# Two-layer LoRA kernel: product 5 of the first span taken by output tile

## The chip, the cores and the metric

The kernel runs on one core of a Trainium2 chip. The metric is the device time of one execution in microseconds (us), as the median over timed runs. Before the change it is 404.14 us (three runs, 402.94 to 404.2 us).

## The reference, cut to what matters

Two layers with a residual each, in float32, on x of 8 batches x 256 tokens x 1024 features:

```
# layer 0
base   = x @ W.T                                   # 1024 x 1024
logits = x @ Wr.T;  logits[.., language] += 5      # 8 experts
gates  = softmax over the top 2 logits, scattered to 8 experts
h      = x @ A.T                                   # 8 experts x rank 16 = 128
x      = x + base + 2 * (h * gates) @ B            # B: 128 x 1024
# layer 1
x      = x + x @ weight[adapter of the batch].T    # 1024 x 1024, chosen per batch
```

## The kernel before, in words

**Precision.** Every large product is made from parts: ScalarE copies an operand to float32r ("high", line 965), VectorE subtracts the copy from the operand ("low", line 583), and TensorE adds high x high, high x low and low x high (the function `step`, lines 1227 to 1229, three matmuls of 128x128 by 512 columns). The identity is added to the weights, so the residual needs no operation of its own.

**Layer 0.** The 2048 tokens go in two spans of 1024 (s = 0, 1). In a span the 1024 x 1024 by 1024 product is done in Strassen's way (Winograd's form) with seven products of 512 x 512 by 512, in the order 1, 2, 6, 7, 5, 4, 3. Each product has four slices k of the contraction and four output tiles r, one PSUM bank per tile: 16 steps, 48 matmuls. "By tile" means that r is the outer loop and k the inner one, so that tile r ends after 4(r+1) steps; otherwise k is outer and all four tiles end in the last four steps. `by_tile` says which: before, products 1, 2 and 6 of span 0. `product_end` and `k_end` turn that into counts of the semaphore `steps`. Products 1, 6, 7 and 4 accumulate in the four "main" banks, products 2, 5 and 3 in the four "side" banks. Sums between products are taken out of PSUM: `copy_u3` (ScalarE, L1007) copies a main bank after product 7, `add_up` (VectorE, L715) adds a side bank to a kept sum and gives one output tile of a quarter of the result (C11, C22, C12), and `keep` (issued from ScalarE's queue, L1017) stores that tile in DRAM. `copy_u2` (L1002) copies main banks after product 6.

**The operands of product 5** are sums as well: S1 (L628, VectorE, one per tile r, in place in the weights) gives the weight side, pieces ("u", 5, r); the token side is pieces ("x", 0, 5, k). The other made operands around are T4 (L620) and D of B (L623, `sum_bd`, with the piece ("bd",), used by the LoRA term of C12 at the end of the span).

**The LoRA term.** VectorE makes the gates (`make_gates`, L650 to L687), TensorE turns h x gates (L1259), ScalarE and VectorE split it (`gT_high` L987, `gT_low` L692), and TensorE adds three matmuls per tile into the bank (`lora`, L1238 to L1241). For C11 that comes between products 7 and 5: the four side banks get the LoRA term, `add_up` reads them, and only then may product 5 begin in the same banks.

**The order around the change** is written by hand, one in-order program per engine. Semaphores `hi_done` and `lo_done` count the pieces, and the list PIECES gives each piece its number, so ScalarE and VectorE must make them in that order. Before, VectorE ended its work ahead of product 5 in this order: gates, low of B, S1(0), gT_low, S1(1), S1(2), low u5(0), S1(3), low u5(1 to 3), low x5(0), the four sums of C11, low x5(1 to 3), D of B, T4 x4, low of D of B, low u4, low x4, the sums of C22. TensorE waited ahead of product 5 for all four u5 pieces and x5(0) (`whole_piece`), and ahead of each tile's first step for its sum of C11.

**Layer 1** then takes the eight batches one after another, each with a 1024 x 1024 weight loaded by DMA, turned and split in the same way (L730, L736, L1066), with its matmuls on lines 1349 to 1351.

Of the kernel before, what the change touches and what calls it, by code (L numbers as in the profile page):

```python
# [5 lines left out]
def cond_resid_kernel(nc, x, lang_ids, adapter_ids, w0, wr, a, b, w1, out):  # L6
# [15 lines left out]
    HM = M // 2  # L22
# [23 lines left out]


    def by_tile(s, i):
        return s == 0 and i in (1, 2, 6)

    def product_end(s, i, r=HM - 1):
        first = 16 * (7 * s + AT[i])
# [44 lines left out]
    PIECES += [("xr", t) for t in range(XT)] + [("wr", 0)]  # L97
    PIECES += [("x", 0, 6, t) for t in range(XT)] + [("u", 6, r) for r in range(HM)]
    PIECES += [("u", 7, r) for r in range(HM)] + [("x", 0, 7, k) for k in range(HM)] + [("b",)]
    for i in (5, 4, 3):  # L100
        PIECES += [("bd",)] if i == 4 else []
        PIECES += [("u", i, r) for r in range(HM)] + [("x", 0, i, k) for k in range(HM)]
    for i in ORDER:
        PIECES += [("x", 1, i, k) for k in range(HM)]
    PIECE_AT = {p: k for k, p in enumerate(PIECES)}
# [21 lines left out]
    with ctx:  # L127
# [407 lines left out]
        def _(dve):  # L535
# [38 lines left out]
            def low(p):  # L574
                dve.wait_ge(hi_done, PIECE_AT[p] + 1)
                if p[0] == "u" and p[1] == 4:
                    dve.wait_ge(s1_done, p[2] + 1)
                if p[0] == "u" and p[1] == 7:
                    dve.wait_ge(s2_done, p[2] + 1)
                if p[0] == "x" and p[2] == 3:  # L580
                    dve.wait_ge(t3_done, (p[1] + 1) * XT)
                _, high_part, low_part = sides(p)
                nc.vector.tensor_tensor(low_part, sides(p)[0], high_part.bitcast(F32), ALU.subtract).then_inc(lo_done, 1)  # L583
# [38 lines left out]
            def sum_bd():  # L622
                nc.vector.tensor_tensor(bd_sum, b_whole[:, 0:HALF], b_whole[:, HALF:D], ALU.subtract)\  # L623
                    .then_inc(bd_summed, 1)

            def make_s1(r):
                a21, a22 = quarter_w(5, r), quarter_w(4, r)
                nc.vector.tensor_tensor(a21, a21, a22, ALU.add).then_inc(s1_done, 1)  # L628
# [61 lines left out]
            def gT_low(s):  # L690
                dve.wait_ge(gT_hi_done, s + 1)
                nc.vector.tensor_tensor(gT_lo, gT_ps(s), gT_hi.bitcast(F32), ALU.subtract).then_inc(gT_done, 1)  # L692
# [6 lines left out]
            def add_up(s, quarter, r):  # L699

                dve.wait_ge(lora_done, quarter_at(s, quarter, r) + 1)
                if quarter == "11":
                    if r < DRAINED:
                        dve.wait_ge(p1_added, DRAINED * s + r + 1)
                    else:
                        dve.wait_ge(p1_copied, HM * s + r + 1)
                elif quarter == "22":
                    dve.wait_ge(u3_copied, HM * s + r + 1)
                else:
                    dve.wait_ge(u2_copied, HM * s + r + 1)  # L710
                e = quarter_at(s, quarter, r)
                if KEPT <= e < quarter_at(1, "12", 0):
                    dve.wait_ge(kept[e % KEPT], e // KEPT * 16)
                part = (sums2 if quarter == "12" else sums13)[:, r]
                nc.vector.tensor_tensor(kept_slot(e), side_bank(s, r), part, ALU.add).then_inc(summed_up, 1)  # L715
# [99 lines left out]
            make_gates(0)  # L815
            low(("b",))
            make_s1(0)
            gT_low(0)
            make_s1(1)
            make_s1(2)  # L820
            low(("u", 5, 0))
            make_s1(3)
            for r in range(1, HM):
                low(("u", 5, r))

            def span(s):
                low(("x", s, 5, 0))
                for r in range(HM):
                    add_up(s, "11", r)
                low(("x", s, 5, 1))  # L830
                low(("x", s, 5, 2))
                low(("x", s, 5, 3))
                if s:
                    turn_w1(0)
                    turn_w1(1)
                    low_w1(0)
                    turn_w1(2)
                    low_w1(1)
                    turn_w1(3)
                else:  # L840
                    sum_bd()
                    for t in range(XT):
                        make_t4(0, t)
                    low(("bd",))
                    lows("u", 4)
                lows("x", s, 4)
                if s:
                    low_w1(2)
                    turn_w1(4)
                    low_w1(3)  # L850
                    turn_w1(5)
                for r in range(HM):
                    add_up(s, "22", r)
                if s == 0:
                    lows("u", 3)
                lows("x", s, 3)
                if s == 0:
                    for t in range(XT):
                        turn(x_item(1, 0, t))
                else:  # L860
                    low_w1(4)
                    turn_w1(6)
                    low_w1(5)
                    turn_w1(7)
                    low_w1(6)
                    low_w1(7)
# [43 lines left out]
        def _(act):  # L910
# [56 lines left out]
            def highs(kind, *which):  # L967
                for r in range(HM):
                    high((kind, *which, r))
# [9 lines left out]
            def exponentials(s):  # L979
                act.wait_ge(drop_ready, s + 1)  # L980
                nc.scalar.activation(second[:], drop[:], ACT.Exp).then_inc(second_ready, 1)
# [137 lines left out]
            for q in range(Q):  # L1119
# [1 line left out]
                                     b_ps().rearrange("p a f -> p (a f)")  # L1121
                                     .rearrange("p (j q m h) -> p q m h j", j=M, q=Q, m=M)[:, q],
                                     ACT.Copy).then_inc(b_copied, 1)
            copy_u2(0, 0)
            copy_u2(0, 1)
            high(("x", 0, 7, 0))
            high(("x", 0, 7, 1))
            copy_u2(0, 2)
            copy_u2(0, 3)
            high(("x", 0, 7, 2))  # L1130
            high(("x", 0, 7, 3))
            high(("b",))
            exponentials(0)
            gT_high(0)

            def span(s):
                if s == 0:
                    highs("u", 5)
                highs("x", s, 5)
                for r in range(HM):  # L1140
                    copy_u3(s, r)
                keep_all(s, "11")
                if s:
                    for n in range(4):
                        high_w1(n)
                else:
                    high(("bd",))
                    highs("u", 4)
                highs("x", s, 4)
                keep_all(s, "22")  # L1150
                if s == 0:
                    highs("u", 3)
                highs("x", s, 3)
                if s:
                    load_x1(0)
                    load_x1(1)
                    high_w1(4)
                    high_w1(5)
                for r in range(HM):
                    copy_c21(s, r)  # L1160
                if s == 0:
                    keep_all(s, "21")
                else:
                    high_w1(6)
                    high_w1(7)
                    x1_high(0)
# [36 lines left out]
        def _(pe):  # L1203
# [64 lines left out]
            def first_products():  # L1268
# [12 lines left out]
                for r in range(HM):  # L1281
# [4 lines left out]
                    if r == 1:  # L1286
                        turn_b()

            def product(s, i, wait_bank, first, bank, ks=range(HM)):
                for k in ks:  # L1290
                    whole_piece(s, i, k)
                    for r in range(HM):
                        if k == 0:
                            wait_bank(r)
                        step(s, i, k, r, bank(s, r), first)

            def span(s):
                if s:
                    product(s, 6, lambda r: pe.wait_ge(p1_copied, HM * s + r + 1), False, main_bank)
                gated = 2 if s else 3  # L1300
                product(s, 7, lambda r: pe.wait_ge(u2_copied, HM * s + r + 1), False, main_bank, range(gated))
                turn_gated(s)
                product(s, 7, None, False, main_bank, range(gated, HM))
                pe.wait_ge(gT_done, s + 1)
                pe.wait_ge(lo_done, PIECE_AT["b",] + 1)
                for r in range(HM):
                    lora(s, "11", r)
                product(s, 5, lambda r: pe.wait_ge(summed_up, added_at(s, "11", r) + 1), True, side_bank)
                for r in range(HM):
                    lora(s, "22", r)  # L1310
                product(s, 4, lambda r: pe.wait_ge(u3_copied, HM * s + r + 1), False, main_bank)
                for r in range(HM):
                    lora(s, "21", r)
                product(s, 3, lambda r: pe.wait_ge(summed_up, added_at(s, "22", r) + 1), False, side_bank)
                pe.wait_ge(lo_done, PIECE_AT["bd",] + 1)
                for r in range(HM):
                    lora(s, "12", r)
# [61 lines left out]
```

## Time and profile before

| what | us |
|---|---|
| median of the timed runs | 404.14 |
| the profiled execution's own time | 401.46 |
| its span | 399.7 |
| PE busy (98% of the span) | 391.1 |
| DVE busy (78%) | 310.2 |
| ACT busy (43%) | 173.8 |

The profile is of one execution. PE is TensorE's matmuls, PEld its weight loads, DVE is VectorE, ACT is ScalarE, POOL is GpSimd, SP is the queue of most loads. ACTq is ScalarE's instruction queue, where it issues DMAs. A matmul's record is 0.39 us long, while the next one may start sooner. Starts are counted from the start of the span, and a later wait is named with the instruction that ended it.

### The profile page before, as it was taken

What the parts mean: (1) busy time and instruction counts of PE and PEld (TensorE: products, weight loads), DVE (VectorE), ACT (ScalarE), POOL (GpSimd) and SP (SyncE); (2) the same over time, 40 slices, a digit from 0 to 9 for tenths busy, and PEclk for the clock granted to TensorE, in tenths of its full rate; (3) what the DMA queues carried; (4) which work ended last, traced back from release to release, by engine and by line L of the source; (5) the groups of instructions that cost most, each with busy time, mean ns of one, the idle gap of its engine ahead of it and who ended that gap; (6) DMA issues with size and microseconds to landing.
All of it is one profiled execution on the core that took longest, in us unless ns stands there. A gap on an engine that the chain in (4) does not pass through costs nothing.

```text
span 399.7 us, 5958 instructions
## 1 busy us (share of the span) xinstructions
PE 391.1 (98%) x1900; PEld 330.0 (83%) x1900; DVE 310.2 (78%) x419; ACT 173.8 (43%) x245; POOL 52.9 (13%) x81
## 2 busy tenths in 40 slices
PE   8899999799999999999999999999999999999996
PEld 8698988588889888888888888878888888888886
DVE  5899998997457568229877956999999999999900
ACT  3352263754220143335355333655555555656511
POOL 1005300000000100000110211442232120323000
PEclk9999999999999999999999999999999999999999
DMA  9998750033476400006492999999999999999232
GB/s 208 227 200 209 106 161 2 0 107 106 137 202 204 91 1 0 2 0 197 136 289 117 229 261 247 281 250 267 271 274 282 266 277 282 272 260 235 66 93 52
DMA packets 87553, 68.60 MB, mean 172 GB/s; under 512 B 16322, under 2 KB 86498, under 8 KB 87010
## 3 DMA queue, kind: packets, MB, share of 16 engines
q1 hardware_dynamic: 60832, 46.55, 49.8%
q10 hardware_dynamic: 26690, 21.67, 18.3%
q8 instruction: 15, 0.25, 0.3%
q14 instruction: 16, 0.13, 0.1%
HBM read 53.51 MB, written 14.68 MB: 171 GB/s over the span
## 4 chain that ended last, share of the span: by engine, by line
PE 94%; DVE 2%; ACT 1%; DMA 1%; issue 0%; ACTq 0%; DVEq 0%
PE banks L1349 15%; PE banks L1350 15%; PE banks L1351 15%; PE banks L1227 13%; PE banks L1228 12%; PE banks L1229 12%; PE banks L1220 7%; PE banks L1238 2%; PE banks L1240 2%; PE banks L1241 2%; DMA turned_w_f<-in_x_dram 1%; DVE weights L583 1%; ACT weights L965 0%; DVE turned_w_f L628 0%; PE banks L1259 0%; DVE tokens_f L545 0%
## 5 line engine op out<-in xcount | busy, mean ns | idle before, releaser
L1227 PE MATMUL banks<-ring,weights 128*128 128x512 f32 x192 | 75.2, 392 | 2.4 <-DVE stage L715 2.4
L1349 PE MATMUL banks<-weights,tokens 128*128 128x512 f32 (+1 forms) x184 | 70.0, 380 | 0.0
L1351 PE MATMUL banks<-weights,tokens 128*128 128x512 f32 (+1 forms) x184 | 69.9, 380 | 0.0
L1350 PE MATMUL banks<-weights,tokens 128*128 128x512 f32 (+1 forms) x184 | 69.9, 380 | 0.0
L1066 ACT ACTIVATE weights<-weights_f 128x1024 fp32r<-128x1024 f32 x44 | 46.5, 1060 | 52.7 <-DVE weights_f L730 49.8
L730 DVE STREAM_TRANSPOSE weights_f<-raw 128x1024 f32<-128x1024 f32 x42 | 51.8, 1235 | 6.1 <-POOL raw L501 5.6
L501 POOL TENSOR_TENSOR raw<-raw,ident 128x128 f32<-128x128 f32 x42 | 26.0, 619 | 216.0 <-DMA raw<-in_L_cond_weight_dram 216.0
L736 DVE TENSOR_TENSOR weights<-weights_f,weights 128x1024 fp32r<-128x1024 f32 x44 | 52.3, 1190 | 0.9 <-ACT weights L1066 0.9
L1229 PE MATMUL banks<-ring,turned_w 128*128 128x512 f32 x128 | 49.8, 389 | 0.0
L1228 PE MATMUL banks<-tokens,weights 128*128 128x512 f32 x128 | 49.8, 389 | 0.0
L1227 PEld LDWEIGHTS banks<-ring,weights 128*128 128x128 f32 x192 | 36.0, 188 | 10.1 <-DVE tokens L583 2.8
L1349 PEld LDWEIGHTS banks<-weights,tokens 128*128 128x128 f32 x184 | 34.6, 188 | 7.0 <-issue 0.4
L1351 PEld LDWEIGHTS banks<-weights,tokens 128*128 128x128 f32 x184 | 34.6, 188 | 6.6
L1350 PEld LDWEIGHTS banks<-weights,tokens 128*128 128x128 f32 x184 | 34.6, 188 | 6.5
L965 ACT ACTIVATE ring<-tokens_f 128x512 fp32r<-128x512 f32 x40 | 22.5, 621 | 29.2 <-PE banks L1229 25.1
L1066 ACT ACTIVATE turned_w<-weights_f 128x1024 fp32r<-128x1024 f32 x20 | 21.2, 1060 | 23.6 <-DVE weights_f L730 23.5
L1349 PE MATMUL banks<-turned_w,tokens 128*128 128x512 f32 x80 | 31.1, 389 | 0.0
L1350 PE MATMUL banks<-turned_w,tokens 128*128 128x512 f32 x80 | 31.1, 389 | 0.0
L1351 PE MATMUL banks<-turned_w,tokens 128*128 128x512 f32 x80 | 31.1, 389 | 0.0
L730 DVE STREAM_TRANSPOSE weights_f<-ring_f 128x1024 f32<-128x1024 f32 x22 | 27.1, 1233 | 5.1 <-POOL ring_f L501 5.1
L1220 PEld LDWEIGHTS banks<-fac,tokens_f 128*128 128x128 f32 x256 | 30.0, 190 | 0.3
L1220 PE MATMUL banks<-fac,tokens_f 128*128 128x136 f32 x256 | 30.1, 279 | 0.0
(127 smaller groups left out, 613.8 us busy)
## 6 DMA issues: line engine op xcount, KB each, us to landing
raw<-in_L_cond_weight_dram SPq DMA_DIRECT2D x168, 128.0 KB, 5.2
ring_f<-in_L_cond_weight_dram SPq DMA_DIRECT2D x88, 128.0 KB, 5.8
out_dram<-sums ACTq DMA_DIRECT2D x31, 256.0 KB, 7.0
raw<-in_x_dram SPq DMA_DIRECT2D x48, 128.0 KB, 3.7
x_kept<-stage ACTq DMA_DIRECT2D x24, 256.0 KB, 3.2
raw<-in_L_cond_W_dram SPq DMA_DIRECT2D x16, 128.0 KB, 3.2
turned_w_f<-in_x_dram SPq DMA_DIRECT2D x12, 128.0 KB, 6.6
ring_f<-in_L_cond_W_dram SPq DMA_DIRECT2D x12, 128.0 KB, 5.4
```

The source lines that it names most:

```text
L501: nc.gpsimd.tensor_tensor(spot, spot, ident[:].rearrange("p (q j) -> p q j", q=Q), ALU.add)\
L730: nc.vector.transpose(w1_turn(n).rearrange("p (m q s) -> p q m s", m=M, q=Q), raw_tile(SLOT[item]).rearrange("p (q m j) -> p q m j", q=Q, ...
L736: nc.vector.tensor_tensor(w1_dest(n, 1), w1_turn(n).rearrange("p (m f) -> p m f", m=M), w1_dest(n, 0).bitcast(F32), ALU.subtract).then_inc ...
L965: nc.scalar.activation(sides(p)[1], sides(p)[0], ACT.Copy).then_inc(hi_done, 1)
L1066: nc.scalar.activation(w1_dest(n, 0), w1_turn(n).rearrange("p (m f) -> p m f", m=M), ACT.Copy)\
L1220: mm = nc.tensor.matmul(ps, xT[:, m, :], fac[:, m, 0:FC], start=m == 0, stop=m == M - 1)
L1227: nc.tensor.matmul(ps, u_hi, x_hi, start=first and k == 0, stop=False, skip_group_check=True)
L1228: nc.tensor.matmul(ps, u_hi, x_lo, start=False, stop=False, skip_group_check=True)
L1229: nc.tensor.matmul(ps, u_lo, x_hi, start=False, stop=k == HM - 1, skip_group_check=True)\
L1349: nc.tensor.matmul(ps, x_hi, w_hi, start=m == 0, stop=False)
L1350: nc.tensor.matmul(ps, x_hi, w_lo, start=False, stop=False)
L1351: mm = nc.tensor.matmul(ps, x_lo, w_hi, start=False, stop=m == M - 1)
```

## The change

Product 5 of span 0 goes by output tile (`product_5`), and tile r waits for ("u", 5, r) and its own sum of C11 alone. VectorE makes x5(0) right after S1(0), and then one set per tile: the sum of C11, S1 and the piece u5. ScalarE makes the x parts of product 7 before its last `copy_u2`, x5(0) before `gT_high`, and `copy_u3` and `keep` of C11 tile by tile. D of B and its parts come after the x parts of product 4 rather than before product 4's parts. Span 1 keeps its order.

```diff
     def by_tile(s, i):
-        return s == 0 and i in (1, 2, 6)
+        return s == 0 and i in (1, 2, 6, 5)
@@ PIECES
-    for i in (5, 4, 3):
+    PIECES += [("x", 0, 5, 0), ("u", 5, 0)] + [("x", 0, 5, k) for k in range(1, HM)] + [("u", 5, r) for r in range(1, HM)]
+    for i in (4, 3):
+        PIECES += [("u", i, r) for r in range(HM)] + [("x", 0, i, k) for k in range(HM)]
         PIECES += [("bd",)] if i == 4 else []
-        PIECES += [("u", i, r) for r in range(HM)] + [("x", 0, i, k) for k in range(HM)]
@@ VectorE
             make_gates(0)
             low(("b",))
             make_s1(0)
+            low(("x", 0, 5, 0))
             gT_low(0)
+            low(("u", 5, 0))
+            low(("x", 0, 5, 1))
+            add_up(0, "11", 0)
+            low(("x", 0, 5, 2))
+            low(("x", 0, 5, 3))
             make_s1(1)
             make_s1(2)
-            low(("u", 5, 0))
+            low(("u", 5, 1))
+            add_up(0, "11", 1)
             make_s1(3)
-            for r in range(1, HM):
-                low(("u", 5, r))
+            low(("u", 5, 2))
+            add_up(0, "11", 2)
+            low(("u", 5, 3))
+            add_up(0, "11", 3)
 
             def span(s):
-                low(("x", s, 5, 0))
-                for r in range(HM):
-                    add_up(s, "11", r)
-                low(("x", s, 5, 1))
-                low(("x", s, 5, 2))
-                low(("x", s, 5, 3))
                 if s:
+                    low(("x", s, 5, 0))
+                    for r in range(HM):
+                        add_up(s, "11", r)
+                    low(("x", s, 5, 1))
+                    low(("x", s, 5, 2))
+                    low(("x", s, 5, 3))
...
                 else:
-                    sum_bd()
                     for t in range(XT):
                         make_t4(0, t)
-                    low(("bd",))
                     lows("u", 4)
                 lows("x", s, 4)
...
+                else:
+                    sum_bd()
+                    low(("bd",))
                 for r in range(HM):
                     add_up(s, "22", r)
@@ ScalarE
-            copy_u2(0, 0)
-            copy_u2(0, 1)
-            high(("x", 0, 7, 0))
-            high(("x", 0, 7, 1))
-            copy_u2(0, 2)
+            for r in range(HM - 1):
+                copy_u2(0, r)
+            highs("x", 0, 7)
             copy_u2(0, 3)
-            high(("x", 0, 7, 2))
-            high(("x", 0, 7, 3))
             high(("b",))
             exponentials(0)
+            high(("x", 0, 5, 0))
             gT_high(0)
+            high(("u", 5, 0))
+            for k in range(1, HM):
+                high(("x", 0, 5, k))
+            for r in range(1, HM):
+                high(("u", 5, r))
+                copy_u3(0, r - 1)
+                keep(0, "11", r - 1)
+            copy_u3(0, HM - 1)
+            keep(0, "11", HM - 1)
 
             def span(s):
-                if s == 0:
-                    highs("u", 5)
-                highs("x", s, 5)
-                for r in range(HM):
-                    copy_u3(s, r)
-                keep_all(s, "11")
                 if s:
+                    highs("x", s, 5)
+                    for r in range(HM):
+                        copy_u3(s, r)
+                    keep_all(s, "11")
                     for n in range(4):
                         high_w1(n)
                 else:
-                    high(("bd",))
                     highs("u", 4)
                 highs("x", s, 4)
+                if s == 0:
+                    high(("bd",))
                 keep_all(s, "22")
@@ TensorE
+            def product_5():
+                for r in range(HM):
+                    pe.wait_ge(lo_done, PIECE_AT["u", 5, r] + 1)
+                    pe.wait_ge(summed_up, added_at(0, "11", r) + 1)
+                    for k in range(HM):
+                        if r == 0 and k:
+                            pe.wait_ge(lo_done, PIECE_AT["x", 0, 5, k] + 1)
+                        step(0, 5, k, r, side_bank(0, r), True)
...
-                product(s, 5, lambda r: pe.wait_ge(summed_up, added_at(s, "11", r) + 1), True, side_bank)
+                if s:
+                    product(s, 5, lambda r: pe.wait_ge(summed_up, added_at(s, "11", r) + 1), True, side_bank)
+                else:
+                    product_5()
```

## Rows read from the trace of the kernel before

**Rows 1.** The page's parts 1 and 4: busy time, and the chain by engine.
```profile
PE 391.1 (98%) x1900; PEld 330.0 (83%) x1900; DVE 310.2 (78%) x419; ACT 173.8 (43%) x245; POOL 52.9 (13%) x81
PE 94%; DVE 2%; ACT 1%; DMA 1%; issue 0%; ACTq 0%; DVEq 0%
```
**Rows 2.** TensorE's waits: who waited for whom, total us, times, longest.
```profile
PE banks L1227 <- DVE stage L715: 2.4, 1, 2.4
PE banks L1206 <- POOL ident L490: 1.7, 1, 1.7
PE banks L1227 <- DVE weights L583: 1.3, 1, 1.3
```
**Rows 3.** Timeline of TensorE, matmuls: start, us, engine, line.
```profile
58.65 0.39 PE L1229 MATMUL banks<-ring,weights 128*128 128x512 f32 x1
60.92 0.39 PE L1227 MATMUL banks<-ring,weights 128*128 128x512 f32 x1
...
73.18 0.39 PE L1241 MATMUL banks<-lora_g,lora_b 128*128 128x512 f32 x1
...
75.22 0.39 PE L1241 MATMUL banks<-lora_g,lora_b 128*128 128x512 f32 x1
78.00 0.47 PE L1227 MATMUL banks<-ring,weights 128*128 128x512 f32 x1 [2.40 <-DVE stage L715]
78.31 0.40 PE L1228 MATMUL banks<-tokens,weights 128*128 128x512 f32 x1
...
88.99 0.39 PE L1238 MATMUL banks<-lora_g,lora_b 128*128 128x512 f32 x1
91.71 0.39 PE L1227 MATMUL banks<-ring,weights 128*128 128x512 f32 x1
```
**Rows 4.** Timeline of VectorE, neighbours of one form merged (xcount).
```profile
59.80 1.29 DVE L583 TENSOR_TENSOR tokens<-tokens_f,ring 128x512 fp32r<-128x512 f32 x2 [0.25 <-ACT ring L965]
62.27 1.29 DVE L583 TENSOR_TENSOR tokens<-tokens_f,ring 128x512 fp32r<-128x512 f32 x2 [1.17 <-ACT ring L965]
...
67.56 1.22 DVE L687 TENSOR_TENSOR stage<-stage 128x1024 f32<-128x1024 f32 x1
...
71.22 1.22 DVE L692 TENSOR_TENSOR lora_g<-banks,lora_g 128x1024 fp32r<-128x1024 f32 x1 [0.70 <-ACT lora_g L987]
72.36 1.28 DVE L628 TENSOR_TENSOR turned_w_f<-turned_w_f 128x512 f32<-128x512 f32 x2
...
76.57 0.69 DVE L583 TENSOR_TENSOR tokens<-tokens_f,ring 128x512 fp32r<-128x512 f32 x1
77.17 2.48 DVE L715 TENSOR_TENSOR stage<-banks,sums 128x512 f32<-128x512 f32 x4
...
87.64 2.49 DVE L583 TENSOR_TENSOR tokens<-tokens_f,ring 128x512 fp32r<-128x512 f32 x4
```
**Rows 5.** Timeline of ScalarE, the same columns.
```profile
59.14 1.16 ACT L965 ACTIVATE ring<-tokens_f 128x512 fp32r<-128x512 f32 x2 [1.28 <-PE banks L1229]
60.20 0.58 ACT L1002 ACTIVATE sums<-banks 128x512 f32<-128x512 f32 x1
...
70.16 1.03 ACT L987 ACTIVATE lora_g<-banks 128x1024 fp32r<-128x1024 f32 x1 [5.22 <-PE banks L1259]
...
73.08 1.23 ACT L965 ACTIVATE weights<-turned_w_f 128x512 fp32r<-128x512 f32 x2 [1.37 <-DVE turned_w_f L628]
```
**Rows 6.** ScalarE's DMA issues of `keep`: duration ns min/median/max.
```profile
L1017 ACTq DMA_DIRECT2D x_kept<-stage x24: 366/424/1112, 79.8 to 202.9; - x24
```
**Rows 7.** Busy time by stretch: PE, PEld, DVE, ACT, POOL, granted clock, DMA share, GB/s.
```profile
75.50:78.00 2.50, 0.11 (x1) 0.03 (x1) 2.50 (x5) 2.14 (x6) 0.00 (x0) 1.00 0.00 0
78.00:400.00 322.00, 318.48 (x1492) 266.86 (x1492) 241.54 (x285) 140.27 (x186) 42.45 (x64) 1.00 0.69 178
```

## The prediction

> **What bounds the kernel now.** I read the page first, then TensorE's waits, then the timelines of the three engines around the longest of them. The page gives PE 391.1 us of a span of 399.7, and the chain of waits runs 94% over PE [rows 1]. So TensorE sets the time, and only what takes idle time out of it, or puts some in, counts. Its waits are three [rows 2]: two at the start of the span, which the change does not touch, and one of 2.4 us for an `add_up` (L715). The timeline places that one between the LoRA term of C11 and product 5: a matmul starts at 75.22, the next only at 78.00 [rows 3]. VectorE is busy in every part of 75.50 to 78.00, ScalarE in 2.14 us of 2.50 [rows 7]: it is not data that is late but VectorE's order, which makes four u5 pieces and x5(0) before the first sum. That sum is the instruction at 77.17, and it releases TensorE [rows 4].
>
> **What the gap costs.** Product 5 has 48 matmuls and is followed by the 12 of the LoRA term of C22, from 88.99 to 91.71 [rows 3]: 2.72/12 = 0.2267 us each when nothing waits. Without the gap product 5 would begin at 75.22 + 0.227 = 75.45 and end 48 x 0.2267 = 10.88 later, at 86.33. It ends at 88.99. The gap is worth 2.66 us, a little more than the 2.4 of the waits, since matmuls restart slowly (78.00 to 78.31 is 0.31, not 0.23). This is the most that the change can give; by tile or by slice the matmuls are as many and of the same shape. By-tile order brings no cost of its own: product 6 is by tile and its last ten steps run from 58.65 to 60.92 at 2.27/10 = 0.227 [rows 3].
>
> **Before product 5.** ScalarE now does copy_u2(2) before x7(0). It stood idle 1.28 us before x7(0) at 59.14 [rows 5], and that x part waits for product 6's step at 58.65 + 0.39 = 59.04. Tile 2 of product 6 ends three matmuls sooner, about 58.36, so the copy (0.58) runs about 58.40 to 58.98, in that idle time, and x7(0) stays near 59.14. This matters, since TensorE starts product 7 at 60.92 and the low part starts at 59.80 [rows 3, 4] and ends 0.69 later, at 60.49: some 0.1 us to spare before the weight load that goes ahead of the matmul. I cost it at nothing; if ScalarE were late by d, it costs d less 0.1. x7(2) and x7(3) move from behind two copies to before the last. Then x7's lows end about 1.4 us sooner (start 62.27 before, about 60.9 after), and the gates with them: 67.56 + 1.22 = 68.78 becomes about 67.4. TensorE turns the gated h only after three slices of product 7, at 69.09 in any case, so this gives no time, and gT_high stays at 70.16 [rows 5] and gT_low at 71.22. What it gives is room: VectorE has x5(0)'s low and S1(0) done by 69.8 and waits for gT_low at 71.22 [rows 4]. copy_u2(3) moves by about 0.2 us to 61.3 and is needed at 62.6 (product 7's tenth matmul): covered.
>
> **Product 5, step by step.** VectorE starts successive instructions of 128x512 0.60 us apart although each lasts 0.69 (four in 2.48, so 2.48 - 0.69 over 3) [rows 4]. ScalarE's high follows the S1 it needs by 0.03 (72.36 + 0.69 = 73.05, start 73.08 [rows 4, 5]), lasts 0.63, and the low follows by 0.03. From the end of a sum to the second matmul of the tile it releases takes 78.31 - (77.17 + 0.69) = 0.45.
> From 72.36: low u5(0) 72.36, low x5(1) 72.96, sum 0 at 73.61 (its LoRA matmul starts at 73.18 and ends 0.39 later [rows 3]), low x5(2) 74.21, low x5(3) 74.81, S1(1) 75.41, S1(2) 76.01. High u5(1) runs 76.13 to 76.76, so low u5(1) starts 76.79 and sum 1 at 77.39, ending 78.07. S1(3) 77.99, low u5(2) 78.59, sum 2 at 79.19 ends 79.87; low u5(3) 80.15, sum 3 at 80.75 ends 81.43. ScalarE has between these a copy_u3 (0.6) and a keep, whose issue takes 0.42 at the median [rows 6], per tile; with both, high u5(2) is ready at 78.4 and high u5(3) at 80.1, as used.
> TensorE: tile 0 needs sum 0 by 75.2 and has it at 74.3. Tile 1's second matmul is due at 75.45 + 13 x 0.2267 = 78.40; the sum allows 78.07 + 0.45 = 78.52. So 0.12 is lost, with 0.02 of restart: 0.15. Tile 2 needs its sum by 80.8 (79.87) and tile 3 by 83.5 (81.43). Gain 2.66 - 0.15 = 2.5.
> The one added wait that can bind is thus tile 1's. Behind it on TensorE is everything. Its cost lies between 0 (VectorE 0.15 quicker) and the 0.7 of the first rival.
>
> **Behind product 5.** It now ends at 86.5, and product 4 begins after 12 LoRA matmuls at 89.2 (91.71 before [rows 3]). T4 x4 starts at 81.35; ScalarE's u4 highs wait for all T4 and start at 83.9, VectorE's u4 lows at 84.5 and x4(0)'s at 86.9, ending 87.6 (before 87.64 + 0.69 = 88.3 [rows 4]). Needed at about 88.9: 1.3 us of room, where there were 3.2. D of B, its high and its low (0.69, 0.63, 0.69) then stand between x4 and the sums of C22, which end at 93.8; the keeps and u3's parts queue behind them and are complete at 97.5, x3(0) at 98.1, against product 3's start near 102.7. Product 5 by tile frees its banks no later, and D of B itself is first used at the end of product 3. Nothing later has a date that does not follow TensorE: the loads of span 1 and the weights of layer 1 wait for slots that are freed behind TensorE's steps, and from 78 to 400 PE has no wait in the list [rows 2, 7]. The gain should stay whole.
>
> **Rule weighed.** The four sums of C11 take 2.48 us with 0.69 for one, so the next starts before the last has ended [rows 4].
> The Trainium skill ("VectorE: DVE Perf Modes", section "The DRAIN you can't avoid") says that the next operation starts only when the pipe has emptied, and lets instructions that are not held start sooner. This trace agrees with the second half; by the first alone the chain would be that of the first rival.
>
> **Rivals.**
> 1. *The tile 1 chain is slower than its neighbours suggest*: with no overlap each VectorE instruction takes 0.69 from start to start, counted from gT_low's end at 72.44. Six of them to the end of S1(1) give 76.58, high u5(1) ends 77.24, S1(2) 77.27, low u5(1) and sum 1 end at 78.65, second matmul 79.10 instead of 78.40: 0.7 lost, gain 1.9, time 402.2. For it: many semaphore handoffs in a new order; against it: the pitch of every merged row. 0.13.
> 2. *No change*: the time is given back later (product 4's 1.3 us of room used up by a late T4 or u4, or the start of product 7 late by d), leaving under 1.2. It needs two of these covers to fail together by over 1.5 us; time 403.6. Speaking for it only that DVE is full from 71 to 90. 0.12.
> 3. *Slower*: the chain per tile paces product 5. Place: tiles 1 to 3. If nothing overlaps and each keep takes the longest issue seen, a tile costs S1 0.69, high 0.63, copy 0.60, issue 1.11 [rows 6], low 0.69, sum 0.69 and 0.1 of handoffs = 4.5 against 2.72 of matmuls; three tiles lose 5.4, less the head start of 0.9 that tile 0's sum has: 4.5, so 1.8 more than the gain, time 406. It decides from 2.72 + 0.9 = 3.6 us per tile on. Against it: the S1s of tiles 2 and 3 are made ahead, and the engines overlap. 0.05.
> That the change does not do what it says I see no way to: the new waits are per tile.
> My forecast has 0.70.
>
> **The numbers.** The profiled execution took 401.46 us, 1.76 above its span; it would take 401.46 - 2.5 = 398.96. The median of the runs shown is 2.68 above the profiled one. Applied to the median, 404.14 - 2.5 = 401.6. The runs spread by 1.3 us, and the lowest less the whole gap is 402.94 - 2.66 = 400.3, the lower end. The upper end takes in rival 1 and part of rival 2: 403.5. About 0.3% (1.2 us) is what a measurement of this kernel tells from no change. Faster: forecast and rival 1, less a little for the spread of the runs, 0.80; same 0.14; slower 0.06.
>
> **What would show it.** Right: in the changed profile TensorE's wait for L715 near 75 is gone or below 0.3 us; product 5's first matmul starts near 75.45, the LoRA term of C22 near 86.5 and product 4 near 89.2; gates' last instruction ends near 67.4; VectorE's first sum of C11 starts near 73.6 and the second near 77.4. Wrong: a new wait on an L583 piece or on L715 at tiles 1 to 3, a gap at 60.9 (product 7) or at 89 (product 4), or a span that is not 2.5 us shorter though the gap is gone.

## The result, and the profile after

| | before | after |
|---|---|---|
| median of the timed runs, us | 403.6 (6 runs, 401.41 to 404.6) | 399.35 (6 runs, 398.84 to 399.8) |
| profiled execution, us | 401.46 | 398.99 |
| its span, us | 399.7 | 397.2 |

The ratio is 0.9899 (95% interval 0.9872 to 0.9926), so the change is faster by 4 us. The forecast was 401.6 with a range of 400.3 to 403.5: the time lies below it. Yet between the two profiled executions the difference is 2.5 us, which is the gain of the forecast. Both facts hold, and the question of the experiments is where the other 1.7 us are.

TensorE's waits in the changed kernel (who waited for whom, us in total, times, longest; L1243, L584 and L716 are L1227, L583 and L715 of before). The wait of 2.4 us [rows 2] is gone:

```profile
PE banks L1222 <- POOL ident L491: 1.7, 1, 1.7
PE banks L1243 <- DVE weights L584: 1.7, 1, 1.7
```

The timeline of its matmuls where [rows 3] had the standstill, and at the ends of products 5 and of the LoRA term:

```profile
75.29 0.39 PE L1257 MATMUL banks<-lora_g,lora_b 128*128 128x512 f32 x1
75.52 0.39 PE L1243 MATMUL banks<-ring,weights 128*128 128x512 f32 x1
...
78.01 0.39 PE L1245 MATMUL banks<-ring,turned_w 128*128 128x512 f32 x1
78.32 0.47 PE L1243 MATMUL banks<-ring,weights 128*128 128x512 f32 x1
78.62 0.40 PE L1244 MATMUL banks<-tokens,weights 128*128 128x512 f32 x1
...
86.57 0.39 PE L1254 MATMUL banks<-lora_g,lora_b 128*128 128x512 f32 x1
...
89.29 0.39 PE L1243 MATMUL banks<-ring,weights 128*128 128x512 f32 x1
```

Product 5 follows the LoRA term at once (75.52, forecast 75.45). Tile 1 starts at 78.32, 0.31 behind its predecessor instead of 0.23, and its second matmul follows after 0.30: 0.15 lost, as worked out. Product 4 starts at 89.29 against 91.71, 2.42 sooner.

VectorE's chain for the same stretch, against [rows 4]:

```profile
66.38 1.23 DVE L688 TENSOR_TENSOR stage<-stage 128x1024 f32<-128x1024 f32 x1
...
71.29 1.22 DVE L693 TENSOR_TENSOR lora_g<-banks,lora_g 128x1024 fp32r<-128x1024 f32 x1 [1.35 <-ACT lora_g L998]
...
73.68 0.69 DVE L716 TENSOR_TENSOR stage<-banks,sums 128x512 f32<-128x512 f32 x1
...
77.49 0.68 DVE L716 TENSOR_TENSOR stage<-banks,sums 128x512 f32<-128x512 f32 x1
...
80.49 0.69 DVE L716 TENSOR_TENSOR stage<-banks,sums 128x512 f32<-128x512 f32 x1
...
86.75 2.49 DVE L584 TENSOR_TENSOR tokens<-tokens_f,ring 128x512 fp32r<-128x512 f32 x4
```

The gates end at 67.6 (forecast 67.4), the first, second and fourth sum of C11 start at 73.68, 77.49 and 80.49 (73.6, 77.4, 80.75), the low part of x4(0) at 86.75 (86.9). ScalarE, against [rows 5], has its copy of tile 2 in what was idle time, and x7(0) stays where it was next to its step:

```profile
58.47 0.60 ACT L1013 ACTIVATE sums<-banks 128x512 f32<-128x512 f32 x1 [0.54 <-PE banks L1245]
59.21 2.20 ACT L976 ACTIVATE ring<-tokens_f 128x512 fp32r<-128x512 f32 x4
```

So nothing in the schedule differs from the forecast by more than 0.3 us. What differs is the kernel before: its profiled execution was not a typical one.

### The profile page after: what moved, and what is told of

Same layout as the page of the kernel before. It is cut to its first block, busy times and chain, and to the rows that moved or that the text cites. A ratio compares the mean times of both kernels' runs of the same rounds, so it can differ in the third digit from the quotient of the medians.

```text
span 397.2 us, 5961 instructions
## 1 busy us (share of the span) xinstructions
PE 390.6 (98%) x1900; PEld 330.0 (83%) x1900; DVE 311.2 (78%) x419; ACT 173.6 (44%) x245; POOL 55.2 (14%) x81
## 4 chain that ended last, share of the span: by engine, by line
PE 96%; DVE 1%; DMA 1%; ACT 1%; ACTq 0%; issue 0%; DVEq 0%
PE banks L1377 15%; PE banks L1378 15%; PE banks L1379 15%; PE banks L1243 13%; PE banks L1244 13%; PE banks L1245 13%; PE banks L1236 7%; PE banks L1256 2%; PE banks L1254 2%; PE banks L1257 2%; DMA turned_w_f<-in_x_dram 1%; DVE weights L584 1%; ACT weights L976 0%; PE banks L1275 0%; DVE tokens_f L546 0%; PE banks L1265 0%
## 5 line engine op out<-in xcount | busy, mean ns | idle before, releaser
L1243 PE MATMUL banks<-ring,weights 128*128 128x512 f32 x192 | 75.5, 393 | 0.0
L502 POOL TENSOR_TENSOR raw<-raw,ident 128x128 f32<-128x128 f32 x42 | 30.3, 722 | 218.3 <-DMA raw<-in_L_cond_weight_dram 218.3
L1243 PEld LDWEIGHTS banks<-ring,weights 128*128 128x128 f32 x192 | 36.1, 188 | 7.9 <-issue 0.3
L1245 PEld LDWEIGHTS banks<-ring,turned_w 128*128 128x128 f32 x128 | 24.0, 188 | 5.0
```

The costliest lines, as they stand in the source:

```text
L502: nc.gpsimd.tensor_tensor(spot, spot, ident[:].rearrange("p (q j) -> p q j", q=Q), ALU.add)\
L1243: nc.tensor.matmul(ps, u_hi, x_hi, start=first and k == 0, stop=False, skip_group_check=True)
L1245: nc.tensor.matmul(ps, u_lo, x_hi, start=False, stop=k == HM - 1, skip_group_check=True)\
```

## The experiments

In each experiment the kernel before was timed on the same chip, and every timed run lists its mean granted clock of TensorE. Counts of runs below are counts of these lists.

**1. The kernel before again.** No edit.

> The kernel before, unchanged, profiled and timed once more. What is asked: the changed kernel's profile shows just the 2.5 us of the forecast (span 397.2 against 399.7), yet the timed runs moved by 4.1 us (ratio 0.990), because most runs of the kernel before took 403 to 404.6 us while the profiled one took 401.46. Theory T1 (a thin cover in the kernel before gives way in most runs: TensorE's turn of h x gates has 0.1 us of room there and 1.3 us after the change): a slower execution shows TensorE waiting at L1259, for 1 to 3 us. Rival T2 (the scatter lies elsewhere, in the loads of the start or of layer 1, and has nothing to do with the change): a slower execution shows its extra time at the start or behind 222 us, with the stretch from 55 to 105 us as in the first profile.

Measured: 403.04 us, ratio 0.9994 (0.9975 to 1.0012). Its profiled execution is a slower one, 403.03 us with a span of 401.2, and shows no wait at L1259 (T1) and nothing new at either end of the span (T2). TensorE's waits are those of [rows 2], the standstill is as long as before, and what follows it is not. Busy time by stretch; the column behind POOL is the granted clock, in this second profile of the kernel before:

```profile
76.00:78.00 2.00, 0.00 (x0) 0.00 (x0) 2.00 (x5) 1.81 (x4) 0.00 (x0) 1.00 0.00 0
78.00:80.00 2.00, 1.78 (x5) 1.42 (x6) 2.00 (x5) 1.83 (x4) 0.00 (x0) 0.59 0.00 0
80.00:82.00 2.00, 2.00 (x7) 1.57 (x6) 2.00 (x4) 0.56 (x1) 0.00 (x0) 0.55 0.54 176
82.00:84.00 2.00, 2.00 (x10) 1.64 (x9) 2.00 (x5) 0.64 (x1) 0.00 (x0) 1.00 1.00 343
```

And its matmuls:

```profile
75.43 0.39 PE L1241 MATMUL banks<-lora_g,lora_b 128*128 128x512 f32 x1
78.22 0.64 PE L1227 MATMUL banks<-ring,weights 128*128 128x512 f32 x1 [2.40 <-DVE stage L715]
78.66 0.63 PE L1228 MATMUL banks<-tokens,weights 128*128 128x512 f32 x1
79.08 0.63 PE L1229 MATMUL banks<-ring,turned_w 128*128 128x512 f32 x1
...
81.22 0.63 PE L1228 MATMUL banks<-tokens,weights 128*128 128x512 f32 x1
81.64 0.46 PE L1229 MATMUL banks<-ring,turned_w 128*128 128x512 f32 x1
81.94 0.40 PE L1227 MATMUL banks<-ring,weights 128*128 128x512 f32 x1
...
90.80 0.39 PE L1238 MATMUL banks<-lora_g,lora_b 128*128 128x512 f32 x1
```

After standing still from 75.66 to 78.22, TensorE works at its lower clock, 1.2 GHz: the first eight matmuls of product 5 take 3.42 us (78.22 to 81.64), 0.427 each instead of 0.227. Then the clock is back at 2.4 GHz. Product 5 takes 90.80 - 78.22 = 12.58 us against 88.99 - 78.00 = 10.99 in [rows 3]: 1.6 us more. Half a clock missing for 3.42 us of 401.2 makes a mean clock of 0.996 over the whole execution, which is what this run lists. In all experiments together 78 runs of the kernel before were listed: 56 have a clock of 0.996 or less, with a median of 403.2 us, and 22 have 0.998 to 1.0, with a median of 401.6. The first profile, with 401.46 us and a clock of 1.00, is like the 22. T1 and T2 both fall, and a third theory, T3, takes their place: the standstill brings the clock down in about 7 executions of 10. So far this is an inference from one profile; experiments 5 to 8 test it.
The Trainium skill ("TensorE: Matmul & The Clock Gate", section "Part 1: The HAM clock gate (the "warmup" mystery)") says that TensorE's clock gate passes only half of the pulses after it has been idle. The trace agrees: the granted clock is 0.59 and 0.55 in the two stretches behind the standstill.

**2. ScalarE's order around product 7 alone**, in the kernel before:

```diff
-            copy_u2(0, 0)
-            copy_u2(0, 1)
-            high(("x", 0, 7, 0))
-            high(("x", 0, 7, 1))
-            copy_u2(0, 2)
+            for r in range(HM - 1):
+                copy_u2(0, r)
+            highs("x", 0, 7)
             copy_u2(0, 3)
-            high(("x", 0, 7, 2))
-            high(("x", 0, 7, 3))
```

> The kernel before with only ScalarE's new order around product 7 (copy_u2(0 to 2), the four x7 parts, copy_u2(3)). In the profile the gap ahead of product 5 stays 2.66 us and the gates end at 67.4 instead of 68.8. T1: the median falls by 1 to 1.6 us (ratio about 0.997), with runs that scatter less. T2: ratio 1.000.

Measured: 403.03 us (401.27 to 405.0), ratio 0.9994 (0.9976 to 1.0012), 9 of 12 runs at 0.996 or less. No gain and no smaller scatter: room for the gates is worth nothing by itself. T1 is rejected.

Its profile (403.04 us) has the same standstill of 2.55 us, from 75.34 to 77.89, and the clock falls behind it too, but later:

```profile
77.89 0.47 PE L1223 MATMUL banks<-ring,weights 128*128 128x512 f32 x1 [2.40 <-DVE stage L715]
...
79.13 0.45 PE L1225 MATMUL banks<-ring,turned_w 128*128 128x512 f32 x1
79.38 0.63 PE L1223 MATMUL banks<-ring,weights 128*128 128x512 f32 x1
...
82.77 0.40 PE L1225 MATMUL banks<-ring,turned_w 128*128 128x512 f32 x1
```

Here the first six matmuls of product 5 are 0.25 apart, and only the next eight (79.38 to 82.77, 0.424 each) run at the lower clock. The granted clock falls to 0.50 at 79.3, 1.4 us after TensorE has begun to work again; in the profile of experiment 1 it is 1.00 through the whole standstill as well and falls at 78.4, 0.2 us after the first matmul.

**3. The changed kernel with ScalarE's old order there** (the same edit the other way round).

> The changed kernel with ScalarE's old order around product 7. The gates end at 68.8, and S1(0) and x5(0) just fit before gT_low at 71.3, so the span stays near 397.2. T1: the median is 1 to 1.6 us above the changed kernel's (ratio to before about 0.993, the forecast's 2.5 us), and runs scatter as before. T2: ratio as the changed kernel's, 0.990.

Measured: 399.31 us, ratio 0.9906 (0.989 to 0.9923), span 397.4, no run below 0.999. That is the changed kernel's time (399.35), so nothing else in the change needs this part.

**4. D of B back where it was**, in the changed kernel:

```diff
                 else:
+                    sum_bd()
                     for t in range(XT):
                         make_t4(0, t)
+                    low(("bd",))
                     lows("u", 4)
...
-                else:
-                    sum_bd()
-                    low(("bd",))
```

> The changed kernel with D of B made where it was (sum before T4, its low before u4). VectorE is then 1.2 us later at u4 and x4(0), about 88.8, and product 4 wants x4(0) at about 88.9 (it starts at 89.3 in the changed kernel): a wait of 0 to 0.5 us, ratio to before 0.990 to 0.991. Both theories alike; it prices the part 'D of B later'.

Measured: 399.49 us, ratio 0.9917 (0.9895 to 0.9939), span 397.4. x4(0)'s low starts at 87.71 instead of 86.75 and ends at 88.40, and TensorE has no wait at product 4, so the 1.3 us of room were enough for it. One of its six runs is at 401.04 us with a clock of 0.995, though this kernel has no standstill ahead of product 5; its profile is of another run (clock 1.0) and does not explain it. What the part gives is below what can be told here.

**5. The standstill filled**, in the kernel before; product 5 starts as late as it did, but TensorE is at work until then.

```diff
                 for r in range(HM):
                     lora(s, "11", r)
+                if s == 0:
+                    for _ in range(10):
+                        extra = nc.tensor.matmul(main_bank(0, HM - 1), bT_hi[:, 0:P], gT_hi[:, 0, :], start=False,
+                                                 stop=True, skip_group_check=True)
+                    extra.then_inc(filled, 1)
```

(ScalarE's copy of that bank waits for `filled`. The ten matmuls add to the bank what does not belong there, so the kernel serves for timing only.)

> The kernel before with ten more matmuls of 128x128 by 512 after the LoRA term of C11, in the bank of tile 3 of product 7 (they add to C11, C12 and C21 of that tile what does not belong there), so that TensorE works for 2.27 us of the 2.55 it stood still. VectorE's chain and the start of product 5 at 78.0 us stay. What is asked: in most runs of the kernel before the granted clock is 0.996 instead of 1.0, and its second profile shows product 5's first eight matmuls 0.427 us apart instead of 0.227 (1.2 GHz), right behind the standstill. Theory T3 (the standstill brings the clock down): no run falls to 0.996, all are near 401.3 us, ratio 0.995. Rival T4 (the clock falls at this point for another reason, and the changed kernel only happens to be spared): the share of runs at 0.996 stays as before (about 7 in 10), ratio 1.000.

Measured: 401.47 us (12 runs, 401.31 to 401.8), ratio 0.9969 (0.9954 to 0.9984); all 12 runs at 0.999 or 1.0, beside 21 of 32 runs of the kernel before at 0.996 or less. The profile of this kernel: ten matmuls that serve nothing, and product 5 behind them, 0.31 and then 0.23 apart, at a granted clock of 1.00.

```profile
75.89 2.43 PE L1313 MATMUL banks<-lora_g,lora_b 128*128 128x512 f32 x10
78.44 0.47 PE L1230 MATMUL banks<-ring,weights 128*128 128x512 f32 x1
78.75 0.39 PE L1231 MATMUL banks<-tokens,weights 128*128 128x512 f32 x1
```

Ten useless matmuls make the kernel before faster by 1.2 us (the ratio) to 1.5 us (the medians). The rival T4 falls: only TensorE's standstill was taken away.

**6 and 7. A standstill put into the changed kernel**, by one wait ahead of product 5:

```diff
             def product_5():
+                pe.wait_ge(s1_done, 3)                                 # only in 6
+                pe.wait_ge(summed_up, added_at(0, "11", 1) + 1)        # only in 7
```

> The changed kernel, where product 5 waits also for S1 of tile 2 (made at 76.8 us): TensorE stands still from 75.5 to 76.9, 1.3 us. T3: the clock falls in fewer runs than with 2.6 us of standstill, perhaps none; span +1.3 to 1.4, median 400.7, ratio 0.993 to 0.994. T4: no fall.

> The changed kernel, where product 5 waits also for the sum of C11 of tile 1 (77.49 + 0.69 = 78.2 us): TensorE stands still for 2.75 us, as long as in the kernel before, while all else is the changed kernel. Only 2.6 us of standstill come back (the 0.2 us wait ahead of tile 1 goes). T3: 7 in 10 runs at clock 0.996 with 1.7 us more, median at that of the kernel before, 403.3, ratio 1.000. T4: no fall, median 401.9, ratio 0.9965.

Measured for 6: 400.67 us, ratio 0.9948 (0.9929 to 0.9967), nine runs, none below 0.998: 1.3 us above the changed kernel's 399.4 in the other comparisons, and 1.3 us is the length of its standstill (75.64 to 76.94), so nothing more is lost. Measured for 7: 403.34 us, ratio 1.0004 (0.9985 to 1.0022), 8 of 12 runs at 0.996 or less. A standstill of 2.70 us (75.50 to 78.20) brings back the time of the kernel before, with everything else as changed. The eight runs with the lower clock have a median of 403.5 us, the four others 401.9. In its profile the stretches around the standstill:

```profile
76.00:78.00 2.00, 0.00 (x0) 0.00 (x0) 1.90 (x4) 1.63 (x3) 0.00 (x0) 1.00 0.38 129
78.00:80.00 2.00, 1.80 (x4) 1.46 (x5) 2.00 (x5) 1.17 (x2) 0.00 (x0) 0.57 0.40 133
80.00:82.00 2.00, 2.00 (x7) 1.55 (x6) 2.00 (x4) 1.20 (x2) 0.00 (x0) 0.58 0.39 132
```

**8. x5(0) early, product 5 by slice.** The kernel before with the edit of experiment 2 and x5(0) made ahead of gT_low (with its high ahead of gT_high, and its number in PIECES):

```diff
             make_s1(0)
+            low(("x", 0, 5, 0))
             gT_low(0)
```

> The kernel before with ScalarE's new order around product 7 and x5(0) made before gT_high and gT_low, as in the changed kernel; product 5 goes by slice and S1, u5 and the sums keep their order. One VectorE instruction of 0.60 us leaves the chain ahead of the first sum: standstill 1.95 us instead of 2.55, span -0.6. T3: the clock falls in fewer runs, so the median falls by more than 0.6: 400.8 to 402.7, ratio 0.994 to 0.9985. T4: -0.6 alone, ratio 0.9985.

Measured: 400.96 us (12 runs, 400.71 to 401.95), ratio 0.9955 (0.9941 to 0.9968), no run below 0.999. Its matmuls at the standstill:

```profile
75.14 0.39 PE L1244 MATMUL banks<-lora_g,lora_b 128*128 128x512 f32 x1
77.32 0.47 PE L1230 MATMUL banks<-ring,weights 128*128 128x512 f32 x1 [1.79 <-DVE stage L716]
```

From 75.37 to 77.32 is 1.95 us. With ScalarE's order of experiment 2, which alone gave nothing, moving one instruction of 0.60 us away from the sums gives 1.8 us (0.45%), somewhat under half of what the whole change gives: 0.6 from the shorter standstill (the runs of before that kept their clock have a median of 401.6, which is 0.65 above 400.96), the rest because the clock no longer falls. The profiled run is one of the slower ones, 401.58; it has a wait of 0.74 us for a token part at 194.72 that the profile before doesn't have.

**9. The changed kernel again.**

> The changed kernel once more, for more executions. T3 (the standstill of 2.6 us ahead of product 5 brings the clock down, and the change gains the standstill and the slow matmuls behind it): no run at a granted clock of 0.996 or less, median 399.3, ratio to before 0.990 to 0.992 as before runs at 0.996 are two thirds or more; against the runs of before that stayed at 1.0 (401.2 to 401.9) the gain is the 2.5 us of the forecast. T4 (chance): some runs at 0.996.

Measured: 399.45 us, ratio 0.9914 (0.9889 to 0.9939), all six runs at 0.999 or 1.0, beside 8 of 11 of the kernel before at 0.996 or less. Those three of before that stayed up took 401.25 to 401.92 us: 1.8 to 2.5 us more.

**10. S1 of tile 1 sooner**, in the changed kernel:

```diff
             add_up(0, "11", 0)
+            make_s1(1)
             low(("x", 0, 5, 2))
             low(("x", 0, 5, 3))
-            make_s1(1)
-            make_s1(2)
             low(("u", 5, 1))
             add_up(0, "11", 1)
+            make_s1(2)
```

> The changed kernel with S1 of tile 1 made right after the first sum, ahead of x5(2) and x5(3), and S1 of tile 2 after the second sum. High u5(1) is then ready at 75.6, the sum of tile 1 starts at 76.7 instead of 77.5, and the 0.07 us wait with its restart (0.15 in all) ahead of tile 1 goes; x5(2) starts at 74.9, wanted at 76.9. Span 397.0, median 0.1 to 0.2 below the changed kernel's, less than the measurement can tell.

Measured: 399.08 us against 399.45 for the changed kernel in the same comparison; ratios to before 0.9909 (0.9883 to 0.9934) and 0.9914, so the two can't be told apart by time. In the profile (span 396.8) tile 1's sum starts early enough that its matmul at 78.18 follows at 0.23, and product 5 takes 86.34 - 75.46 = 10.88 us, the 48 x 0.2267 of the forecast without any loss:

```profile
75.46 0.39 PE L1243 MATMUL banks<-ring,weights 128*128 128x512 f32 x1
...
78.18 0.39 PE L1243 MATMUL banks<-ring,weights 128*128 128x512 f32 x1
...
86.34 0.39 PE L1254 MATMUL banks<-lora_g,lora_b 128*128 128x512 f32 x1
```

## Why the prediction was right or wrong

**Right: the schedule.** The standstill's 2.66 us, the 0.15 us left at tile 1, the 1.3 us of room at product 4 (D of B later), the cover of copy_u2(2), and that nothing behind gives the gain back: the profiled spans differ by 2.5 us as worked out. Rival 1 (no overlap on VectorE) is excluded by the second sum at 77.49, rival 3 by the fourth at 80.49, rival 2 by product 4 at 89.29 and by the span, which keeps the gain to the end. That the early x7 parts give room but no time was right too (experiments 2 and 3). One word is wrong and changes nothing: what runs from 58.65 to 60.92 are the last ten matmuls of product 6, not ten steps.

**Wrong: a term that was left out.** The step that failed is the sentence in "What the gap costs": "The gap is worth 2.66 us ... This is the most that the change can give". In about 7 executions of 10 the same standstill also halves TensorE's clock for some 3.4 us behind it, and that costs 1.6 us more (12.58 against 10.99 us for product 5). So the gain on a typical execution is 2.5 + 1.6 = 4.1 us. The measured difference of the medians is 403.6 - 399.35 = 4.25. From the longer lists it is 403.2 (the 56 runs of before at the lower clock) - 399.4 (the 12 of the changed kernel) = 3.8, and without the clock's part, 401.6 (the 22 that stayed up) - 399.4 = 2.2. Where in an execution the clock falls is seen in three profiles (experiments 1, 2 and 7), each time behind the standstill; of the other runs only the mean clock and the time are known, and both fit. Experiment 5 takes the clock's part alone away (ratio 0.9969), experiment 7 puts both back (ratio 1.0004), experiment 6 shows a shorter standstill that costs its own length only.

Of the 2.25 us between the forecast of 401.6 and the 399.35 measured, this term is 1.6. Another 0.5 was in the starting point: the median of three runs was 404.14, that of six is 403.6 (and that of the 56 is 403.2). The lower end of the range, 402.94 - 2.66 = 400.3, lacks the same term.

**Why it was missed.** The trace of before showed the clock at 1.00 on both sides of the gap [rows 7], and I took that execution for the kernel. (Behind the gap that row is a mean over 322 us, in which 3.4 us at half clock would be 0.5%; it is the 10.99 us of product 5 that show that this execution had no fall.) But the forecast itself notes that the median of the runs shown is 2.68 us above the profiled execution, and passes over it as spread, by moving the result up with it: 404.14 - 2.5. The runs were 402.94, 404.2 and 404.14 and the profiled one 401.46. A profile faster than every run beside it may be from the faster of two groups, and the standstill of [rows 2, 3] was its one long one behind the start. Both together suggest a rival that the prediction should have had: what makes the typical run longer than the profiled one hangs on the gap and goes with it. Its time needs no further price: it is the profiled execution less the gain, 401.46 - 2.5 = 398.96, which stands in the prediction and was put aside for 401.6. Measured: 399.35.

**What stays open.** Why the clock stays up in 3 of 10 runs with the same standstill was not tried, nor why the fall came at once in two profiles and later in that of experiment 2, nor where one run of experiment 4 lost its clock. Within one group the runs of before still spread by about 1 us. TensorE's waits for VectorE's first weights (L583, 1.1 and 1.3 us in two profiles of before, 1.7 after) vary by part of that; I did not follow it further.

## What to carry to other kernels

A wait of TensorE costs its length and, from some length on, what the next matmuls lose at the lower clock; here 2.6 us of standstill cost about 4 in most executions, 1.95 us cost nothing beyond itself. So shortening a wait can pay more than it removes, and filling it with work that serves nothing can pay as well. Before a gain is worked out from one profile, compare that execution's time and clock with the timed runs: where they form two groups, ask which group the profile shows and what the change does to the other.

## What the hardware showed unexpectedly

How often the clock falls changed within a narrow range of the standstill's length, with matmuls of the same shape on both sides. Runs at a mean clock of 0.996 or less: none of 12 in the changed kernel (no standstill there) and one of 18 in its variants without a standstill (experiments 3, 4 and 10), none of 9 with 1.3 us, none of 12 with 1.95 us, 56 of 78 with 2.55 us and 9 of 12 in experiment 2 with the same length, 8 of 12 with 2.7 us. In three profiles with the fall (experiments 1, 2 and 7) the granted clock is still 1.00 while TensorE stands still; it falls 0.1 to 0.2 us after the first matmul behind the standstill in two, and 1.4 us after it in one. Each time it comes back 3.4 us later, while TensorE works on.
